# Two attention layers and two expert layers on one core: routing of one batch moved into the attention of the other, and routing of the other between experts

## The reference

```python
capacity = int(Sz * 2.0 / E) + 1                      # 257
scores = softmax(einsum('bsd,ed->bse', x, router_w))  # E = 8 experts
gate_vals, sel_idx = top_k(swapaxes(scores, 1, 2), capacity)   # every expert takes 257 tokens of each batch
tokens = x[b_idx, sel_idx]
y = gelu(tokens @ w1 + b1) @ w2 + b2                  # 128 -> 512 -> 128
out = zeros_like(x).at[b_idx, sel_idx].add(y * gate_vals[..., None])
```

## Time and profile before

| what | us |
|---|---|
| median of 3 runs | 986.13 (985.75 to 987.85) |
| the profiled execution | 991.8, its span 990.1 |
| layer 0, start of the expert stage to the first product of an expert | 339.98 to 404.96 |
| layer 0, experts to the last gates | 404.96 to 496.69 |
| layer 1, the same two | 820.49 to 880.28, 880.28 to 971.97 |
| TensorE, VectorE, ScalarE, GpSimd busy | 842.2, 681.5, 484.7, 325.2 |

### The profile page before, as it was taken

The page is one execution under the profiler, slowest core; times in us unless marked ns, Lnnn a source line. Parts: engine busy times, 40 slices in busy tenths (PEclk is TensorE's granted clock), DMA queues, the critical chain, the costliest instruction groups (busy, mean ns, idle before and its releaser), DMA issues. The chain is left out here.

```text
span 990.1 us, 17157 instructions
## 1 busy us (share of the span) xinstructions
PE 842.2 (85%) x6146; PEld 543.8 (55%) x6146; DVE 681.5 (69%) x1751; ACT 484.7 (49%) x1044; POOL 325.2 (33%) x563
## 2 busy tenths in 40 slices
PE   1888999999999865899957888999999987679994
PEld 0554566556655543799944433444444435369993
DVE  3886667777774457988564876777777645698864
ACT  0614566666666530355404255666666674035551
POOL 1080135444221430255526111233212334034554
PEclk9998999999999979799969598999999998979996
DMA  9481120111000230024235271110000005002335
GB/s 265 103 281 33 33 55 11 34 33 33 2 1 2 60 111 4 3 23 70 26 56 127 66 190 36 34 33 10 25 2 2 2 1 171 1 6 20 47 44 107
DMA packets 58484, 53.56 MB, mean 54 GB/s; under 512 B 6224, under 2 KB 51424, under 8 KB 58016
## 3 DMA queue, kind: packets, MB, share of 16 engines
q1 hardware_dynamic: 43968, 43.60, 16.3%
q0 software_dynamic: 9216, 4.20, 4.8%
q10 hardware_dynamic: 5216, 4.66, 1.6%
HBM read 28.40 MB, written 22.94 MB: 52 GB/s over the span
## 5 line engine op out<-in xcount | busy, mean ns | idle before, releaser
L997 ACT ACTIVATE b_pt<-b_banks 128x512 f32<-128x512 f32 (+1 forms) x320 | 154.8, 559 | 103.8 <-PE b_banks L911 103.6
L1020 DVE TENSOR_REDUCE a_mlate<-a_banks 128x2 f32<-128x1024 f32 (+3 forms) x120 | 124.7, 1079 | 49.6 <-PE a_banks L849 31.1
L1020 DVE TENSOR_REDUCE b_mlate<-b_banks 128x2 f32<-128x1024 f32 (+3 forms) x120 | 126.1, 1080 | 37.0 <-PE b_banks L859 19.0
L1259 POOL DMA_INDIRECT scratch_sum<-f_yg,f_index x64 | 99.4, 1553 | 103.1 <-DVE f_yg L1635 92.1
L911 PE MATMUL a_banks<-a_q,a_k 121*128 121x512 f32 (+3 forms) x384 | 117.1, 383 | 3.6 <-DMA a_q<-a_mt 2.7
L997 ACT ACTIVATE a_q_hl<-a_banks 128x512 f32<-128x512 f32 (+1 forms) x160 | 81.7, 557 | 65.2 <-PE a_banks L911 63.7
L911 PE MATMUL b_banks<-b_q,b_k 64*128 64x512 f32 (+3 forms) x384 | 99.4, 423 | 12.8 <-ACT b_pt L997 8.8
L849 PE MATMUL a_banks<-a_k,a_q 120*128 120x512 f32 (+3 forms) x384 | 99.4, 361 | 11.6 <-DVE a_mlate L1020 7.6
L997 ACT ACTIVATE a_k_hl<-a_banks 128x512 f32<-128x512 f32 (+1 forms) x160 | 82.1, 557 | 53.5 <-PE a_banks L911 52.0
L911 PEld LDWEIGHTS b_banks<-b_q,b_k 64*128 64x128 f32 x384 | 47.8, 191 | 88.1 <-ACT b_pt L997 55.5
L911 PEld LDWEIGHTS a_banks<-a_q,a_k 121*128 121x128 f32 x384 | 65.2, 191 | 48.6 <-issue 20.2
(11 more groups left out here) (243 smaller groups left out, 1453.9 us busy)
## 6 DMA issues: line engine op xcount, KB each, us to landing
scratch_sum<-zero SPq DMA_DIRECT2D x4, 1024.0 KB, 9.5
f_raw<-in_w SPq DMA_DIRECT2D x16, 256.0 KB, 4.6
f_w<-in_w SPq DMA_DIRECT2D x16, 256.0 KB, 4.8
f_sums<-scratch_sum SPq DMA_DIRECT2D x8, 512.0 KB, 4.0
a_q<-scratch_q SPq DMA_DIRECT2D x8, 384.0 KB
a_k<-scratch_k SPq DMA_DIRECT2D x8, 384.0 KB
scratch_q<-b_q_hl SPq DMA_DIRECT2D x24, 128.0 KB, 3.0
b_q<-scratch_q SPq DMA_DIRECT2D x32, 96.0 KB
```

What stands on the lines that cost most here:

```text
L997: act.activation(pt[at % NPT][:, h, 0:cols], st[u % NST][:, 0:cols], ACT.Exp, scale=scale).then_inc(exp_done, 1)
L1020: last = dve.tensor_reduce(dst, src, AX.X, ALU.max, negate=True)
L1259: pool.indirect_dma_start(sums_out[to], at(index[:, q, half:half + 1]), yg[q % NRING][:, half, :], None, compute_op=ALU.add).then_inc(scat ...
```

## The change

Batch 0's routing moves into batch 1's half of the attention ahead of it: projection or join, norm, transposes and router products into half 8, softmax and first count into half 9, and the 30 steps, ties and places beside units from half 9 to half 14 or 15. A long half has eight such sites and a short one three. The sums of the counts go into unused rows of `o_ps` (the search has its 64 rows at partitions 16 to 31 of each 32), so `values` waits until VectorE has read the latest sum. The `keep_busy` products of the expert stage go.

In the expert stage the experts of batch 0 start once batch 1's router products are issued. Batch 1's search runs in 36 ticks between batch 0's experts: on TensorE after the hidden layer, after each half of the picking and after the second and fourth product of the output; on VectorE between pairs of flags. Only the 16-bit flags are left on VectorE (all tiles and 258 columns, three buffers); ScalarE makes the fp32r one-hot from them (`widen`). The hidden layer has three PSUM banks in place of four. Batch 0's edge and final sums are added among batch 1's experts.

```diff
+AT = {"a": {"attn": (8, 10), "through": (8, 12), "normed": (8, 22), "logits": (8, 24), "rows": (9, 2), "spots": (15, 1)},
+      "b": {"normed": (8, 23), "logits": (8, 25), "rows": (9, 3), "spots": (15, 5)}}
+LONG, SHORT = {"a": (0, 8, 11, 14, 16, 19, 22, 25), "b": (0, 4, 12, 14, 17, 20, 22, 25)}, {"a": (0, 8, 11), "b": (0, 2, 5)}
...
+    def step(self, dve, i, c):
+
+        bit = BITS[i]
+        dve.wait_ge(self.totalled, i + 1)
+        dve.tensor_scalar(self.drop[:, :], c[:, 0:1], CAPACITY - 0.5, float(1 << bit), ALU.is_lt, ALU.mult).then_inc(self.read, 1)
+        dve.wait_ge(self.read, i + 1)
+        self.link(dve, dve.scalar_tensor_tensor(out=self.trial[:, :], in0=self.drop[:, :], scalar=(1 << bit) >> 1,
+                                                in1=self.trial[:, :], op0=ALU.bitwise_or, op1=ALU.bitwise_xor))
+        if i + 1 < len(BITS):
+            self.count_above(dve)
+            return
...
+            if summed[0]:
+                pe.wait_ge(route.read, summed[0])
             for key, q0, w, col in set_tiles(c, s)[0]:
...
-            if q >= 3:
+            if e >= 3:
                 pe.wait_ge(gated, 2 * (q - 2))
...
+        def experts(b):
+            q0 = b * NE
+            for half in range(2):
+                pick(q0, half)
+            meta_of(q0)
+            if not b:
+                route.turn_rows(pe, m, s_ps).then_inc(route.rowed, 1)
+            for e in range(NE):
+                q = q0 + e
+                for j in range(HB):
+                    hidden(q, j)
+                tick(b)
+                for half in range(2 if e + 1 < NE else 0):
+                    pick(q + 1, half)
+                    tick(b)
+                if e >= 2:
+                    turn_y(q - 2)
+                for j in range(HB if e else 0):
+                    output(q - 1, j)
+                    if j % 2:
+                        tick(b)
+                if e + 1 < NE:
+                    meta_of(q + 1)
...
+        def widen(q):
+
+            act.wait_ge(flag_ready, QT * (q + 1))
+            if q >= 2:
+                act.wait_ge(x_picked, 2 * (q - 1))
+            act.activation(hot[q % 2][:, :, :], flag[q % NFLAG][:, :, :], ACT.Copy).then_inc(hot_ready, 1)
...
+        def experts(b):
+            q0 = b * NE
+            for e in range(NE):
+                q = q0 + e
+                for i in range(QT // 2):
+                    if i < (3 if e == 0 else QT // 2 if e + 1 < NE else 2):
+                        tick(b)
+                    if e + NFLAG < NE:
+                        flags(q + NFLAG, (2 * i, 2 * i + 1))
+                if e:
+                    tick(b)
+                if e >= 2:
+                    gates(q - 2)
+                if e + 1 < NE:
+                    meta_copy(q + 1)
...
+        flags(1)
+        dve.wait_ge(logits_ready, 2)
+        route.peaks(dve, l_ps[:, 0:QT * NE])
+        flags(2)
...
+        experts(0)
+        for q in range(NE, NE + NFLAG):
+            flags(q)
+            if q == NE:
+                meta_copy(q)
+        experts(1)
```

More of the change, by code:

```diff
@@ L169, in ring_table @@
                 place["o", i - 1] = len(place)
-            if kind == "a" and (i, v) in PROJECT:
-                place["p", PROJECT[i, v]] = len(place)
+            for name, unit in AT[kind].items():
+                if unit == (i, v):
+                    place[name] = len(place)
     place["o", len(HALVES) - 1] = len(place)
@@ L1274, in gpsimd @@
             scatter(q)
+            if q in (0, 1):
+                lower_matrix(NRING + 2 + q)
+            if q in (2, 3):
+                lower(q)
     def tensor(pe):
@@ L1621, in flags @@
+        def flags(q, some=range(QT)):
+            b, e = divmod(q, NE)
+            for t in some:
+                if t == 0 and q >= NFLAG:
+                    dve.wait_ge(indexed, q - NFLAG + 1)
+                    dve.wait_ge(hot_ready, q - NFLAG + 1)
+                col = spot_column(t, e)
+                dve.tensor_scalar(flag[q % NFLAG][:, t, :], m.slot[:, :], spot_t[b][:, col:col + 1], None, ALU.is_equal
                                   ).then_inc(flag_ready, 1)
@@ new lines, in experts @@
+        def experts(b):
+            q0 = b * NE
+            for e in range(NE):
+                q = q0 + e
+                for i in range(QT // 2):
[3 more added lines that the diff above has]
+                        flags(q + NFLAG, (2 * i, 2 * i + 1))
+                if e:
+                    tick(b)
+                if e >= 2:
+                    gates(q - 2)
+                if e + 1 < NE:
+                    meta_copy(q + 1)
+                if b and e == 3:
+                    edge_hots(1)
+                    edge_masks(1)
+                if b and e == 2:
+                    edge_gates(0)
+                if b and e == 3:
+                    edge_scale(0)
+                if b and e in (4, 5):
+                    edge_add(e - 4)
+                    finish(e - 4, 0)
+                    finish(e - 4, 1)
+            if b:
+                edge_gates(1)
+            gates(q0 + NE - 2)
+            gates(q0 + NE - 1)
+            while not b and ticks[0] < NTICK:
+                tick(b)
@@ L1690, in vector @@
-        edge_scale(0)
-        gates(WORK - 1)
+        dve.wait_ge(route.rowed, 1)
+        link(dve.tensor_copy(route.rows, s_ps))
+        route.count_above(dve)
+        edge_hots(0)
+        edge_masks(0)
+        experts(0)
+        for q in range(NE, NE + NFLAG):
+            flags(q)
+            if q == NE:
+                meta_copy(q)
+        experts(1)
         edge_scale(1)
-        for c in range(NCH):
+        for c in (2, 3):
             edge_add(c)
-        for b in range(B):
-            for half in range(2):
-                finish(b, half)
+        for half in range(2):
+            for c in (2, 3):
+                finish(c, half)
```

734 lines of the change are left out of this document (405 added, 329 removed).

## The result

The changed kernel takes 1097.34 us (median of 4 runs, 1091.84 to 1117.11) against 986.99 us for the kernel before beside it: ratio 1.110, 95% interval 1.104 to 1.115, so 110 us slower. The profiled execution takes 1095.53 us, its span is 1093.8. The forecast was 1003, range 974 to 1024: the sign was right, the size too small by 94 us, and the time lies far outside the range.

A forecast was written before the change was run, and what follows sets the result against it. The prediction took a serial search chain to bound the prologues and TensorE the experts. Terms -84.6 (prologues), +41.5 (attention) and +60.6 (experts) gave +17.5 us, so 1003 us; own range 990 to 1022, over all cases 974 to 1024.

The forecast's parts named there:

- The prologues: Stretches before each layer's experts: taking the serial search out saves 43.9 us in layer 0 and 40.7 in layer 1.
- the widening: ScalarE's widening of an expert's 16-bit flags, 2064 columns: taken at 1.8 us, between 1.6 and 2.2.
- The steps in kind a: Search steps in kind a's attention: values wait for VectorE's read of the sum, +6.0 us per long half, about +1.2 per short.
- the walk: Half 10 of kind a followed through its timeline: values start 2.8 us late after unit 15, then 3.2 us late.
- The steps in kind b: Search steps in kind b's attention: the same walk gives 4.7 us per pair of halves, 9.4 in all, plus 0.4.
- Half 8: Batch 0's routing head in each attention: 26.1 us of VectorE work in 17.4 us, so TensorE waits, +8.7 us each.
- The experts: Expert stage: batch 0 +15 us, change of batches +10.3, batch 1 +3, flags beside GpSimd +2; 30.3 per layer.
- rival (3): Slower still: GpSimd's subtractions hold up flags among the experts, 12.6 us more, 1016, or 1034 with attention at 60; chance 0.12.
- the accumulator's form: Skill rule that VectorE instructions writing an accumulator out do not exclude GpSimd: search steps would be undisturbed by the masks.
- The change of batches: From expert 7 to expert 8, nothing prepared between batches: 16 us against 5.7, +10.3, between 8 and 12.
- (1): Faster: the experts' steps hide, 6.1 us per batch 0 expert instead of 8.3, 981 or 976 us; chance 0.13.
- (2): Faster: the attention's waits cost nothing, 15 us instead of 41.5, 977 us; chance 0.10.

The follow-up runs named there:

- The filler run: The changed kernel plus filler multiplications on TensorE ahead of the waiting sums and values in kind b's attention, no wait removed: 1081.16 us, 1.096 of the kernel before.
- the run with steps first: The changed kernel with each search step of the attention put ahead of its unit's pieces, not behind them: 1051.16 us, 1.065 of the kernel before.
- the fills with zero: The changed kernel with GpSimd's subtractions among the experts replaced by zero fills that read no SBUF operand: 1086.48 us, 1.099 of the kernel before.

## Why the prediction was right or wrong

| term | forecast | measured |
|---|---|---|
| prologues, layer 0 and 1 | -43.9, -40.7 | -41.8, -38.3 |
| half 8, kind a and b | +8.7, +8.7 | +15.7, +14.7 |
| steps, kind a: halves 10 and 12; 11 and 13 | +6.0 each; +1.2 each | +5.9 each; +1.3, +0.8 |
| kind a: halves 9 and 14, steps and projections | +1.5 - 1.5 | +1.3, -2.1 |
| steps, kind b: halves 10 and 11, 12 and 13; halves 9 to 15 | +4.7 a pair; +9.8 | +25.8, +25.2; +56.2 |
| experts, layer 0 and 1 | +30.3, +30.3 | +46.0, +44.5 |
| attention b ahead of half 8 | 0 | -5.6 |
| sum on the span | +17.5 | +103.7 |

The measured column is from the two profiled executions. Of the 5.6 us that attention b gained ahead of half 8, 4.8 are its half 1 (27.7 us before, 23.0 after), where TensorE waited 2.7 us for a transfer in the kernel before. No edit touches it, and the profiled execution before is itself 5 us above its median, so this row is taken as chance, which one trace of the kernel before can't settle.

**The prologues** were right to 2.4 us each. So were the window of the earlier trace rows as the measure of what goes, and the widening (1.9 us, taken at 1.8).

**The steps in kind a** were right in the mechanism, the values wait for the read of the sum, and in the total (6.0 us per long half against 5.9), but the total is partly luck. Measured from the start of half 10, the values after unit 15 come 2.2 us later than before the change and those after unit 23 another 2.6 us, where the walk had 2.8 and 3.2. The rest, 1.1 us, comes behind them, with waits at the sums themselves (0.51 and 0.78 us) that the walk did not have.

**The steps in kind b are the step that failed**: "In kind b values come every fourth unit in smaller bursts and pieces lie one unit later, and the same walk gives 0.55, 0.3, 1.3 and 1.1 us". It is 46 of the 86 us missing by the profiled executions (2.7 of the 46 stay in half 9 when the steps are left out, and belong to the head). Two things were left out. The walk asked when VectorE has read a sum, not when TensorE may form the next one: with the piece one unit later and two sites two units apart, the sum itself waits 1.6 to 2.2 us. And the products were priced at full clock; with those waits most of them ran at 1.2 GHz. The filler run separates the two (the waits filled and not removed, the clock back: half 10 at 34.3 us with 66 extra products), the run with steps first removes both (24.7 us).

**Half 8** had the right mechanism and was too small by 7.0 and 6.0 us. VectorE's extra work was 13.1 us in kind a (forecast 13.5). Not priced were TensorE's own products of the head (five groups in that half of kind a, three in kind b; two of them are worth 0.4 and 2.9 us) and the hand-over behind the overload. In kind a VectorE works without a pause to 239.5 us, then stands idle for 3.2 us while TensorE turns and routes: the two engines' extra work comes one after the other. Against the kernel before, TensorE stands idle 7.1 us more in half 8 of kind a and 4.9 us more in kind b (one wait of 3.4 us for the normalised rows, in which the clock falls to 0.50). These waits are the term that was forecast, at 8.7. It is also busy 8.6 and 9.8 us more, with the products of the head and a mean clock of 0.91 and 0.73, and that had no term. How this part divides among products, clock and hand-overs is open.

**The experts** were right in kind. The wait of the slot numbers for the gates is there (1.48 us), expert 2 took 8.15 us (forecast 8.3), and taking the gates forward gives it 7.03. Experts 3 to 6 took 41.5 us in layer 0 where 33.2 was forecast: each has one VectorE instruction held for about 2 us beside GpSimd's subtraction, and the fills with zero give 7.0 us back of these 8.3. That is rival (3) in kind, which had five holds of 1.26 us on flags; the prediction had taken the steps for undisturbed, by the accumulator's form, and overlooked the trial instruction. The change of batches was 20.6 us against 16, since the widening of expert 9 stood ahead of the copy of expert 8, and ScalarE's order had not been walked there. Experts 0 and 1 took 4.5 us more than before the change, where 1.9 was forecast, and batch 1 5.4 more, where +3 was; its own parts, 0.3 x 8 + 2.9 - 1.74, give 3.6.

**The rivals.** (1) and (2) are excluded by the rows above. (3) gave the sign and a part of the experts' excess; even its 1034 us, the highest time that the prediction names, is 63 us short. No rival named the clock in the attention. "The most uncertain is the walk through a half" was true, but the bound put on it, 60 us for both attentions, took each wait at its own length only; measured were 28.7 us in kind a and 70.9 in kind b from half 8 on.

## What to carry to other kernels

When a step of a serial chain is put beside other work, walk both directions of its hand-over: when the consumer may read, and when the producer may go on. Put the step on each engine ahead of work that the other engine has still to feed. Price a stall of TensorE twice: by its length, and by what follows at the lower clock; kind b lost about as much to the second. If VectorE takes on small instructions with two operands in SBUF, keep GpSimd's reading instructions away from them, or do these on VectorE itself.

## What the runs showed of the hardware

- In half 10 of kind b, with waits of 1.97 and 1.47, 1.61 and 1.47, and 2.19 and 1.54 us, TensorE's granted clock was 0.62 in the mean and 0.50 (1.2 GHz) for long stretches, although no single wait was above 2.2 us. In half 10 of kind a, with 1.70 and 1.51 us as its longest waits, it was 1.00 (2.4 GHz). Small fillers in the waits alone brought kind b back to 1.00. What exactly tips it was not tested.
- A VectorE instruction on 128x1 numbers took up to 2.24 us beside a GpSimd subtraction of 128x512, and 0.16 beside a fill of the same size. With the subtraction cut in four parts it still took 1.54 to 2.02 us.
- The same subtraction took 1.26 us on GpSimd (four in 5.04 us), 1.86 where it followed scatters and held VectorE up, and 0.69 us on VectorE.
